# Unread matmuls in TensorE's idle stretches, and an out projection of one PSUM bank per pair of token groups in the last attention pass

## The reference

```python
h = cond_block(x, cond)         # adaLN, attention of 16 heads of 128, MLP of 1024 with exact GELU
x = x + min_gru(h)              # two 256x256 products, gates, a scan along each sequence
q = rk4_scan(cond, cond, x)     # 32 time steps, 4 stages each: q - q^3/3 - p + drive + tanh(q) @ coupling.T
x = x + sparse_mlp(q)           # router picks 4 of 16 blocks of a 1024 wide MLP
```

## Time and profile before

| | us |
|---|---|
| median of three runs | 493.47 |
| lowest, highest | 492.81, 495.36 |
| the profiled execution | 493.39 |
| its span, first to last instruction | 491.6 |
| PE busy | 463.7 (94%) |
| PE weight loads busy | 333.7 (68%) |
| DVE busy | 389.8 (79%) |
| ACT busy | 320.1 (65%) |
| POOL busy | 48.5 (10%) |
| mean granted clock of TensorE | 0.986 of full |

### The profile page before, as it was taken

One profiled execution on the slowest core, in us unless ns is written; L12 is line 12 of the kernel. 1 busy time (PEld: TensorE's weight loads), 2 busy tenths in 40 slices (PEclk: granted clock), 3 DMA queues, 4 the chain that ended last, 5 costly groups with the idle time before them and its releaser, 6 DMA issues.

```text
span 491.6 us, 13509 instructions
## 1 busy us (share of the span) xinstructions
PE 463.7 (94%) x5126; PEld 333.7 (68%) x5126; DVE 389.8 (79%) x1368; ACT 320.1 (65%) x952; POOL 48.5 (10%) x79
## 2 busy tenths in 40 slices
PE   2999999999999999998789999799999999999997
PEld 2655666558656666567535444698988888888886
DVE  4969885778768877889997997777788887888874
ACT  2577963788377956887476965465666656666573
POOL 3010240223020320224000000000000000000000
PEclk9999999999999999999999999688999999999999
DMA  8982510110101000000000000000000000000000
GB/s 294 419 355 66 131 34 32 55 30 22 65 22 43 21 0 1 1 2 1 0 1 1 1 0 1 1 3 0 1 2 11 11 0 11 0 11 11 1 11 23
DMA packets 10127, 20.85 MB, mean 42 GB/s; under 512 B 1456, under 2 KB 4720, under 8 KB 9456
## 3 DMA queue, kind: packets, MB, share of 16 engines
q1 hardware_dynamic: 9536, 19.89, 11.5%
q10 hardware_dynamic: 560, 0.60, 0.4%
HBM read 19.40 MB, written 1.08 MB: 42 GB/s over the span
## 4 chain that ended last, share of the span: by engine, by line
PE 78%; DVE 11%; ACT 6%; issue 2%; DMA 1%; POOL 1%; ACTq 0%; DVEq 0%
PE bank L857 48%; PE score L857 26%; PE spare L857 2%; ACT ptx L612 2%; DVE big L1552 2%; DVE pairs_store L1597 1%; DMA vec<-vecs 1%; ACT ao_sb L570 1%; DVE ao_sb L1552 1%; PE bank L888 1%; ACT sraw L605 1%; POOL ptx L495 1%; DVE npos L1794 1%; DVE acc L1614 1%; DVE acc L1430 0%
## 5 line engine op out<-in xcount | busy, mean ns | idle before, releaser
L857 PE MATMUL bank<-x,pairs_store 128*128 128x512 f16 x384 | 86.0, 379 | 0.0
L857 PEld LDWEIGHTS bank<-x,pairs_store 128*128 128x128 f16 x384 | 37.2, 98 | 41.9
L495 POOL TENSOR_TENSOR ptx<-pt,ptx 32x256 f16<-32x256 f32 x64 | 44.2, 690 | 181.4 <-ACT ptx L612 177.8
L857 PE MATMUL score<-cub,neg_eye 128*128 128x64 f32 x256 | 57.4, 307 | 0.0
L570 ACT ACTIVATE big<-bank,head_b 128x512 f16<-128x512 f32 x60 | 39.7, 685 | 19.1 <-PE bank L857 18.7
L1889 DVE TENSOR_TENSOR thlo<-th 128x64 f16<-128x64 f32 x128 | 28.8, 225 | 29.2 <-ACT th L784 27.9
L857 PE MATMUL bank<-pairs_store,ao_sb 128*128 128x256 f16 x384 | 46.1, 273 | 4.5 <-DVE ao_sb L1552 2.6
L857 PE MATMUL score<-th,coup_part 128*128 128x32 f16 x1024 | 46.8, 178 | 1.2
L857 PEld LDWEIGHTS bank<-pairs_store,ao_sb 128*128 128x128 f16 x384 | 36.1, 98 | 12.0 <-DVE ao_sb L1552 4.9
L783 ACT ACTIVATE th<-score 128x64 f16<-128x64 f32 x96 | 21.5, 224 | 34.8 <-PE score L857 32.1
L857 PE MATMUL bank<-pairs_store,x 128*128 128x512 f16 x192 | 43.4, 379 | 0.0
(11 more groups left out here) (227 smaller groups left out, 1024.8 us busy)
## 6 DMA issues: line engine op xcount, KB each, us to landing
wqk_sb<-wqk SPq DMA_DIRECT2D x16, 256.0 KB, 3.4
wv_sb<-wv SPq DMA_DIRECT2D x4, 512.0 KB, 5.4
wo_sb<-wo SPq DMA_DIRECT2D x4, 512.0 KB, 4.3
f_sb<-ffn_w SPq DMA_DIRECT2D x2, 1024.0 KB, 14.2
ao_sb<-xtok SPq DMA_DIRECT2D x4, 256.0 KB, 5.8
big<-ada_w SPq DMA_DIRECT2D x1, 1024.0 KB, 9.2
x_sb<-xT SPq DMA_DIRECT2D x1, 1024.0 KB, 13.1
w_sb<-w1T SPq DMA_DIRECT2D x1, 1024.0 KB, 15.7
```

What stands on the lines that cost most here:

```text
L495: nc.gpsimd.tensor_tensor(ptx[s, 1, :, s], pt[s], ptx[s, 0, :, s], ALU.subtract).then_inc(ptx_ready, 1)
L857: return nc.tensor.matmul(dst, lhsT, rhs, start=start, stop=stop, **kw)
```

## The change

It has three parts.

1. *Unread matmuls.* At the start of PE's program 20 of 128 columns (once the bf16 identity is ready) and 12 of 512 columns (once the scaled identity is ready) go into `spare`, before PE waits for the small loads. Before the scan's loop 29 follow the seeding one instead of 18. In the loop, stages 0, 1 and 2 get 2, 5 and 5 of 128 columns behind their fill, into bank 4. The ones of the tail write `score` and bank 4 instead of `spare`.
2. *One bank per c in the last pass.* `LAST_OUT` gives one bank for c = 0, 1 and 2 with two or three use numbers each, which are all emptied at once, and c = 3 takes `spare`, with two semaphores of its own. All four heads accumulate there. The four `add_heads(0, c)` of the last pass go. `gate_heads` and `close_heads` move: for c = 0 and 1 to the end of the third pass, for c = 2 and 3 to the start of the last.
3. *Orders in the last pass.* For head 2 the strips are copied half by ACT and half by DVE too, ahead of the placing of head 1, and DVE's `shift(2)` comes ahead of `low_pv(0)`. `normalise(2)` comes ahead of `low_pv(1, [0])`, and `low_pv(1, [0])` ahead of the last strips. The low strips of head 3 are made half by POOL and half by DVE (`place_last_low`). The split of MLP block 4 moves forward on ACT and DVE.

```diff
-LAST_OUT = [[24, 25, 28, 33], [29, 30, 34, 35]]
+LAST_OUT = [(24, 29, 34), (25, 30, 35), (28, 33)]
...
+        UNREAD_AT = {0: 2, 1: 5, 2: 5}
...
@@ gpsimd, place_low(j)
-                    for q in range(NB4):
+                    for q in range(NB4 // 2 if i == NQUAD - 1 and j == QUAD - 1 else NB4):
...
@@ scalar
-                empty_values(6, 7)
+                empty_values(6)
+                if last:
+                    mlp_highs(4, 5)
+                empty_values(7)
...
                 empty_pv(0)
-                place_high(1)
-                copy_scores(2)
-                empty_projs(3, (0, 1, 2))
                 if last:
-                    mlp_highs(4, 5)
+                    copy_scores(2, NB4 // 2)
+                    place_high(1)
+                    empty_projs(3, (0, 1, 2))
+                    exps(2)
+                    empty_projs(3, [3])
...
@@ tensor
+            pe.wait_ge(ident_ready, 1)
+            for _ in range(20):
+                mm(spare[:, 0:P], ident[:], ident[:], True, True)
+            pe.wait_ge(eye_ready, 1)
+            unread(spare[:], 12)
             pe.wait_ge(small_loaded, 48)
...
@@ out_project
-                    dst = fill(use) if first else bank[bank_of(use)]
+                    if last:
+                        first, end = first and pair == 0, end and pair == 1
+                        if c < len(LAST_OUT):
+                            dst = fill(LAST_OUT[c][0]) if first else bank[bank_of(LAST_OUT[c][0])]
+                            filled, uses = full[bank_of(LAST_OUT[c][0])], len(LAST_OUT[c])
+                        else:
+                            dst, filled, uses = spare, last_full, 1
...
             turn_x2(0)
-            unread(spare[:], 6)
+            unread(score[:, 0], 6)
             turn_normed(0)
-            unread(spare[:], 8)
+            unread(fill(USE_F1[0][3])[:], 8)
...
-            unread(bank[bank_of(USE_F2[1] + 1)][:], 18)
+            unread(bank[bank_of(USE_F2[1] + 1)][:], 29)
...
                     fill_in(i, n, FILL[n][early:])
+                    for _ in range(UNREAD_AT.get(n, 0)):
+                        mm(bank[NBANK - 1][:, 0:P], scaled_eye[:], scaled_eye[:], True, True)
...
@@ vector, take_heads(c)
+                if c < len(LAST_OUT):
+                    use = LAST_OUT[c][-1]
+                    dve.wait_ge(full[bank_of(use)], (NQUAD - 1) * NPAR + count_of(use))
+                    V.tensor_tensor(heads_of[c % 2], bank[bank_of(use)][:], gate_of(c), ALU.mult
+                                    ).then_inc(free[bank_of(use)], len(LAST_OUT[c]))
+                else:
+                    dve.wait_ge(last_full, 1)
+                    V.tensor_tensor(heads_of[c % 2], spare[:], gate_of(c), ALU.mult).then_inc(last_taken, 1)
...
+                def place_last_low():
+
+                    use = LAST_PV[QUAD - 2] + 1
+                    dve.wait_ge(full[bank_of(use)], i * NPAR + count_of(use))
+                    dve.wait_ge(high_placed, i * (QUAD * NB4) + QUAD * NB4)
+                    for q in range(NB4 // 2, NB4):
+                        s = slice(q * T, (q + 1) * T)
+                        V.tensor_tensor(ptx[s, 1, :, s], pt[s], ptx[s, 0, :, s], ALU.subtract).then_inc(ptx_ready, 1)
...
@@ vector, one pass
-                low_values(0, 1)
-                if i == NQUAD - 1:
+                if last:
+                    gate_heads(2)
+                    close_heads(2)
+                    low_values(0)
+                    gate_heads(3)
+                    low_values(1)
                     mlp_lows(0, 1)
+                else:
+                    low_values(0, 1)
...
                 low_weights(i, 7)
-                low_pv(0)
-                shift(2)
...
                 if last:
-                    last_strips()
+                    last_strips(2)
+                    shift(2)
+                    low_pv(0)
+                    low_projs(3)
+                    normalise(2)
+                    low_pv(1, [0])
+                    last_strips(3)
                     shift(3)
                     low_pv(1, [1])
                     normalise(3)
-                    add_heads(0, 0)
                     low_pv(2, [0])
-                    add_heads(0, 1)
+                    place_last_low()
                     low_pv(2, [1])
-                    add_heads(0, 2)
+                    low_pv(3)
...
                     add_heads(1, 1)
+                    if i == NQUAD - 2:
+                        gate_heads(0)
+                        close_heads(0)
                     low_first_head(2, (i + 1) * QUAD)
+                    if i == NQUAD - 2:
+                        gate_heads(1)
                     low_first_head(3, (i + 1) * QUAD)
                     add_heads(1, 2)
+                    if i == NQUAD - 2:
+                        close_heads(1)
                     add_heads(1, 3)
                 if last:
-                    gate_heads(0)
-                    close_heads(0)
-                    low_pv(3)
-                    gate_heads(1)
-                    close_heads(1)
                     take_heads(0)
...
-                    add_heads(0, 3)
                     take_heads(2)
...
             scale_turned(0, 0)
-            gate_heads(2)
             shift_turned(0, 0)
```

More of the change, by code:

```diff
@@ L877, in ada_chunks, with unread @@
                 return last
+            def unread(dst, count):
+                for _ in range(count):
+                    mm(dst, scaled_eye[:], ptx[:, 0, 0:G // 2].rearrange("p g n -> p (g n)"), True, True)
+            pe.wait_ge(ident_ready, 1)
[3 more added lines that the diff above has]
+            unread(spare[:], 12)
             pe.wait_ge(small_loaded, 48)
@@ L972, in values @@
                              ).then_inc(full[bank_of(use)], 1)
-                use_pv, use_out = (LAST_PV, LAST_OUT) if last else (USE_PV, USE_OUT)
+                use_pv = LAST_PV if last else USE_PV
                 def mix(j):
@@ L1006, in out_project @@
                             pe.wait_ge(split_ready, i * NSPLIT + SPLIT_ORDER.index(("o", 1)) + 1)
-                    dst = fill(use) if first else bank[bank_of(use)]
+                    if last:
[6 more added lines that the diff above has]
+                    else:
+                        dst = fill(USE_OUT[pair][c]) if first else bank[bank_of(USE_OUT[pair][c])]
+                        filled, uses = full[bank_of(USE_OUT[pair][c])], 1
                     for g in (2 * c, 2 * c + 1):
@@ L1013, in out_project @@
                             mm(at, hi, wo_pair[:, 1, j], False, False, skip_group_check=True)
-                            last = mm(at, lo, wo_pair[:, 0, j], False, end and n == len(js) - 1, skip_group_check=True)
+                            done = mm(at, lo, wo_pair[:, 0, j], False, end and n == len(js) - 1, skip_group_check=True)
                     if end:
-                        last.then_inc(full[bank_of(use)], 1)
+                        done.then_inc(filled, uses)
                 values(0, 1)
@@ L1609, in add_heads @@
                 def add_heads(pair, c):
-                    use = (LAST_OUT if last else USE_OUT)[pair][c]
+                    use = USE_OUT[pair][c]
                     a = pair_of(c)
@@ L1622, in _ @@
                 low_values(3, 4)
+                if last:
+                    close_heads(3)
                 low_weights(i, 4)
@@ L1659, in _ @@
                     normalise(3)
[L1660 removed]
                     low_pv(2, [0])
[L1662 removed]
+                    place_last_low()
                     low_pv(2, [1])
[L1664 removed]
+                    low_pv(3)
                 else:
+                    low_pv(0)
+                    shift(2)
+                    for k in range(4):
+                        if k == 3:
+                            low_weights(i + 1, 0)
+                        low_proj(3, k)
+                    low_pv(1, [0])
+                    normalise(2)
                     low_pv(1, [1])
@@ L1709, in _ @@
             scale_turned(0, 0)
-            gate_heads(2)
             shift_turned(0, 0)
-            dve.wait_ge(free[bank_of(LAST_OUT[1][2])], (NQUAD - 1) * NPAR + count_of(LAST_OUT[1][2]) + 1)
-            ln.wait()
+            heads_taken(2)
             scale_turned(0, 1)
@@ L1822, in _ @@
                 hidden_low(0, m)
-            dve.wait_ge(free[bank_of(LAST_OUT[1][3])], (NQUAD - 1) * NPAR + count_of(LAST_OUT[1][3]) + 1)
-            ln.wait()
+            heads_taken(3)
             for k in range(KB):
```

52 lines of the change are left out of this document (22 added, 30 removed).

## The result

| | before | after |
|---|---|---|
| median of the runs, us | 494.06 (6 runs) | 488.7 (6 runs) |
| lowest, highest | 492.81, 495.53 | 487.32, 490.2 |
| the profiled execution, us | 493.39 | 487.7 |
| its span, us | 491.6 | 485.9 |
| mean granted clock of it | 0.986 | 0.996 |

The ratio is 0.9883, with a 95% interval of [0.9851, 0.9915]: by it 5.8 us less, between 4.2 and 7.4 (the two medians lie 5.4 apart). Forecast were 487.3 in a range of 485.0 to 490.8.

What follows compares the result with a forecast made beforehand. The prediction blamed half-clock TensorE stretches in the loop's recurrence, paid in full, plus waits in the last pass and a slow-clock start. Sum: 493.4 - 3.5 (scan) - 2.0 (last pass) - 0.6 (start) = 487.3 us, range 485.0 to 490.8.

Steps and rivals of the forecast that it cites:

- The scan's clock: Loop over 32 time steps: keeping TensorE's clock full in the first two rounds gives -3.5 us, ends 0 and 3.9.
- the filled hole: Idle TensorE time before the loop: eleven more unread products keep the clock up, saving 2.4 us in the first round.
- the twelve: Unread products in stages 0 to 2 of each loop round: prevent the second clock dip, worth 1.1 us.
- The 0.1 us left for VectorE's drive rows: First loop round: 0.1 of the 2.5 us gain was set aside for VectorE's work on these rows.
- rival (c): Loop: the clock falls all the same despite the unread products, 490.8 to 490 us; chance 0.09.
- The twelve on the recurrence: Loop stages 0 to 2: the added unread products fit into slack and cost 0, at most 5.4 us.
- rival (d): Loop: the twelve lie on the recurrence and cost their whole length, making the kernel slower at 501 us; chance 0.04.
- The slack: Loop stages 1 and 2: time left behind the five unread products before they delay the recurrence, 0.1 us.
- the rate of 81 ns: Loop: the skill's time per 128-column product; the five would overrun by 0.02 us or more a stage, sum 0.3 to 0.8 worse.
- The last pass: Last attention pass and tail: shared banks, moved ops and new orders start the hidden layer earlier, -2.0 us, ends +0.5 and -2.8.
- The start: Start of TensorE's program: unread products raise the clock early and speed up the transposes, -0.6 us, ends +0.5 and -1.3.
- rival (a): Start of the kernel: the unread products there give nothing or lose a little, 487.9 to 488.5 us; chance 0.2.

Runs made afterwards that it cites:

- no_twelve: bridge_two without the twelve unread products a round in the scan: 488.48 us, ratio 0.9873.
- pass_only: The kernel after without any new unread products, only the last pass changed: 492.11 us, ratio 0.9937 to before.
- double: The kernel after with twice the unread products a round (4, 10 and 10 in stages 0 to 2): 489.69 us, ratio 0.9887.
- no_start: The kernel after without its 32 unread products at the start: 489.21 us, ratio 0.9869.
- after_again: The kernel after, unchanged, run once more on another occasion: 487.78 us, ratio 0.9852.
- start_only: The kernel before with only the 20 and 12 unread products at the start added: 493.84 us, ratio 0.9985.
- bridge_two: bridge with one more unread product behind each 8 of the 24 later small products at the start: 487.48 us, ratio 0.9839.
- bridge: The kernel after with six more unread products between the small products and the transposes at the start: 488.04 us, ratio 0.9862.
- banks_clean: bridge_two with the old orders of the last pass, keeping shared banks and moved gates and MLP weights: 487.38 us, ratio 0.9843.
- scan_only: The kernel before with 29 instead of 18 unread products ahead of the loop and the twelve a round: 490.05 us, ratio 0.9916.
- old_pass: bridge_two with the whole last pass of the kernel before, all unread products kept: 489.26 us, ratio 0.9882.

## Why the prediction was right, and where it was off

**The scan's clock** (term -3.5): right in size and mechanism. The rows give -2.50 for the first round and -1.07 for the second, -3.57 in all; the 0.05 a round after it, which would make it -3.87, is scatter. The split was nearly right: the filled hole is worth 2.1 beside the twelve (2.4 foreseen), the twelve 1.0 to 1.1 beside the filled hole (1.1 foreseen). But the fall that they prevent is not tied to 339.44: in no_twelve it came at 313.90, and in pass_only, which has none of them, there was no second one. The 0.1 us left for VectorE's drive rows in the first round wasn't needed. No half clock was seen in the loop in either profiled run of the kernel after, as forecast, so rival (c) is out; it comes back when either half is taken away.

**The twelve on the recurrence** (cost 0, rival (d) 501): the cost is 0. Rounds of 20.50 exclude (d). The slack that I gave as 0.1 us behind the five is 0.17, by `double`. By the rate of 81 ns of the Trainium skill ("TensorE: Matmul & The Clock Gate", Back-to-back issue gap) the five would have cost 0.02 us or more a stage; the stages got no longer (1.25 and 1.51 in both kernels), so the spacing of this trace, 0.056, was the one to use.

**The last pass** (term -2.0): -1.73 measured. Nearly every step came within 0.3 us of its place: maximum of the third head 214.54 (foreseen 214.6), out projections 222.50 (222.5), head 2's mix ending 226.62 (226.5), strips 229.71 (229.75), head 3's mix ending 231.62 (231.35), low parts 232.15 (232.05), first gated result 233.89 (233.7), hidden layer 246.28 (246.1). What I weighed wrongly is which part pays: most of my working went into the orders, and with the shared banks in place they are worth 0.16. Head 1's low part, now behind head 2's normalising, starts on VectorE at 221.69 and lasts 0.71, and TensorE waits 1.06 us before the out projections; of the 2.08 us by which head 2's maximum comes earlier little is left at the end. Head 3's mix waits for a bank all the same (0.65 us). The bank that the pairs share and the ops that were moved with it are worth ten times as much.

**The start** (term -0.6): this is the step that failed in the profiled execution, which gained 0.04 us at the first projections: rival (a), by a way that the working of the term named. The clock did rise early, and fell again behind the wait for the tokens, at 12.36. Runs at mean clock 1.0 took 0.2 to 0.5 us less than the profiled 487.7, but none of them was profiled. Over the runs the size of the term stays open: no_start is 1.4 us over after_again in the median and start_only 0.9 under before (0.8 and 0.7 by the ratios), neither beyond its scatter. I took one trace's start for the kernel's. With nine more products in the two weak places (bridge_two) the full clock stayed in all six runs; the 32 and the nine together are worth up to 1.7 us against no_start. The nine without the 32 were not tried, so what the 32 add to them is not shown.

I had set against this term the rule of the Trainium skill ("TensorE: Matmul & The Clock Gate", Part 4) that transposes do not engage the full clock. The trace still disagrees. The timeline of PE of the kernel before, right behind its transposes:

```profile
15.69 1.05 PE L857 MATMUL spare<-big,cond_sb 128*32 128x256 f32 x4
```

These four products ran at full clock, where the same four took 1.79 us at half in no_start, and ahead of them TensorE had done nothing but products of 32 columns and transposes. The clock rose while it did those. (The profile lists the transposes as MATMUL; in what mode of TensorE they ran, no row shows.)

**The sum**: 487.3 was forecast for a typical run, 487.7 is the profiled one and 487.2 to 487.5 those at mean clock 1.0. That the profiled one comes so near is in part luck: the last pass missed by 0.3 and the start by 0.6, and 0.3 of that was made up by the scatter of the six later rounds. The median of the six runs, 488.7, lies 1.4 over the forecast, since five of them have, by their mean clock, one or two low stretches (at the start in the two executions that were profiled), which a forecast from a single execution does not hold. The Trainium skill ("TensorE: Matmul & The Clock Gate", Part 1) says that the number of slow products at the start varies from run to run of one kernel. The traces agree: the same twelve unread products of 512 columns, started at 4.85 or 4.86, took 3.07 us in after, 3.12 in after_again, 3.40 in bridge_two and 3.66 in no_twelve, whose programs are the same up to there.

## What to carry to other kernels

A kernel whose times scatter by 1% may be paying for TensorE's clock: find the thin places of TensorE's work ahead of each low stretch (an idle wait, or a stretch of very short products) and fill all of them, since with one left open the low stretch can move there, as it did in bridge. Beside a recurrence, double the filling once and read off how much slack it had. And when an order of work is rearranged together with a buffer, try the old order with the new buffer first: here the buffer, with the ops that were moved beside it, gave nine tenths of the gain.

## What the runs showed that was not expected

Most of the scatter of these kernels goes with the clock. The kernel before ran from 491.85 to 498.44 us on three chips, with mean clocks from 0.993 to 0.973; bridge_two and banks_clean, at 0.999 or 1.0, ran from 487.26 to 487.61 on two. The median of bridge_two is 0.3 us under after_again on the same chip, which alone could be scatter, but its spread is 0.27 us against 3.1.

The clock is not all of it. scan_only ran in 489.58, 489.65 and 490.97 us at mean clock 1.0; in the profile of the slowest of these TensorE's first small products could start only at 10.16, when the small loads had come, against 8.91 in before. The profile of no_start has 10.29. In the other runs it is 8.5 to 9.5. No experiment held the arrival of the loads fixed, so its share in the scatter is open.

A stretch of short products can be a weak place as well as idle time. Ahead of the low stretch at 19.77 in start_only TensorE was busy without a gap, most of the time on 24 products of 32 columns, and so it was ahead of that at 22.22 in no_start; in bridge, at 19.31, there was a gap of 0.35 us behind them. With three products of 512 columns among and behind them no run of bridge_two, banks_clean or old_pass, 15 in all, had a mean clock under 0.999.

The clock's record does not show a low clock before it has first risen: the window from 0 to 12.50 us of before reads 1.00, while its products are 0.226 us apart. So a mean clock leaves out the slow products at the very start, and kernels without unread products there look better by it than they are; four runs of no_start at "1.0" took 487.88 to 489.56.
